# Four batch units in a row at the head of every round, in an interaction kernel with halved turns and double raw slots

## The reference

```python
e = jnp.stack([tbl_0[ids[:, 0]], ..., tbl_31[ids[:, 31]]], axis=1)
p = x[:, iu, :]
q = x[:, ju, :]
result = jnp.einsum('bpe,fpe,bpf->bp', p, kernel, q)
...
h = jnp.concatenate([z, dense_ctx], axis=1)
h = jnp.maximum(h @ W_top1 + b_top1, 0.0)
h = jnp.maximum(h @ W_top2 + b_top2, 0.0)
y = h @ W_top3
```

## Time and profile before

| | |
|---|---|
| runs | 496.06 us median of 3 (494.4 to 496.16) |
| the profiled execution | 494.39 us, span 492.6 us |
| TensorE, VectorE, ScalarE, GpSimd busy | 409.6, 355.8, 346.4, 241.9 us |
| VectorE's instructions | 367 |
| gathers | 256, 944 ns each |

### The profile page before, as it was taken

The page is one execution under the profiler, slowest core; times in us unless marked ns, Lnnn a source line. Parts: engine busy times, 40 slices in busy tenths (PEclk is TensorE's granted clock), DMA queues, the critical chain, the costliest instruction groups (busy, mean ns, idle before and its releaser), DMA issues.

```text
span 492.6 us, 8787 instructions
## 1 busy us (share of the span) xinstructions
PE 409.6 (83%) x2416; PEld 196.9 (40%) x2416; DVE 355.8 (72%) x367; ACT 346.4 (70%) x2661; POOL 241.9 (49%) x260
## 2 busy tenths in 40 slices
PE   0164999899797899999998899999998899999948
PEld 0031434343342444554333344644333354554226
DVE  0041899899786887659889886758988987668950
ACT  1000179989969859885997986789599689759802
POOL 5777777777027777771017777772017770000000
PEclk9995999999998999999999999999999999999979
DMA  3235354421001111110001111110001110000000
GB/s 93 77 102 174 98 183 150 130 53 29 3 6 27 26 28 27 28 27 8 2 5 28 28 28 25 27 28 13 1 5 27 28 28 3 0 2 3 0 1 0
DMA packets 11849, 19.16 MB, mean 39 GB/s; under 512 B 5013, under 2 KB 5913, under 8 KB 11673
## 3 DMA queue, kind: packets, MB, share of 16 engines
q0 software_dynamic: 8192, 8.40, 8.9%
q1 hardware_dynamic: 2592, 8.42, 4.8%
q10 hardware_dynamic: 1016, 1.78, 1.1%
HBM read 18.58 MB, written 0.00 MB: 38 GB/s over the span
## 4 chain that ended last, share of the span: by engine, by line
PE 38%; issue 20%; DVE 19%; ACT 10%; POOL 9%; DMA 2%; DVEq 0%; ACTq 0%; POOLq 0%
ACT prod_a L296 9%; POOL raw L250 9%; PE t_ps L437 9%; PE z_ps L493 8%; PE t_ps L515 6%; DVE prod_a L385 6%; PE t_ps L455 6%; DVE prod L359 4%; PE t_ps L523 3%; DVE zb L399 3%; PE prep_ps L469 2%; DMA raw<-tbl,ids_sb 2%; DVE prod_d L385 2%; PE t_ps L442 2%; DVE prod L363 2%
## 5 line engine op out<-in xcount | busy, mean ns | idle before, releaser
L250 POOL DMA_INDIRECT raw<-tbl,ids_sb x256 | 241.7, 944 | 164.4 <-issue 75.6
L296 ACT ACTIVATE prod_a<-prod_a 128x64 f32<-128x64 f32 x1296 | 309.4, 243 | 2.2 <-ACT y_sb L317 1.2
L296 ACT ACTIVATION_READ_ACCUMULATOR prod_a<-prod_a 128x1 f32 x1296 | 245.3, 189 | 0.0
L437 PE MATMUL t_ps<-xt,k_sb 64*128 64x256 f32 x448 | 129.2, 404 | 23.1 <-DVE prod_a L385 23.0
L359 DVE TENSOR_TENSOR prod<-t_ps,xt 128x1024 f32<-128x1024 f32 x96 | 116.3, 1212 | 41.2 <-PE t_ps L438 39.5
L455 PE MATMUL t_ps<-k_sb,xt 64*128 64x512 f32 x256 | 141.0, 632 | 0.6 <-issue 0.6
L457 PE MATMUL t_ps<-k_sb,xt 64*128 64x512 f32 x256 | 141.0, 632 | 0.0
L438 PE MATMUL t_ps<-xt,k_sb 64*128 64x256 f32 x448 | 129.2, 404 | 0.0
L437 PEld LDWEIGHTS t_ps<-xt,k_sb 64*128 64x128 f32 x448 | 77.9, 190 | 114.2 <-DVE prod_a L385 61.3
L385 DVE TENSOR_TENSOR prod_a<-t_ps,raw 128x1024 f32<-128x1024 f32 x81 | 97.9, 1209 | 0.0
L438 PEld LDWEIGHTS t_ps<-xt,k_sb 64*128 64x128 f32 x448 | 77.9, 190 | 0.0
(11 more groups left out here) (29 smaller groups left out, 216.8 us busy)
## 6 DMA issues: line engine op xcount, KB each, us to landing
raw<-tbl,ids_sb POOLq DMA_INDIRECT x256, 2.5
w_sb<-w ACTq DMA_DIRECT2D x1, 1024.0 KB
k_sb<-kmat SPq DMA_DIRECT2D x1, 992.0 KB, 7.0
k_sb<-kmat SPq DMA_DIRECT2D x1, 896.0 KB
k_sb<-kmat SPq DMA_DIRECT2D x1, 864.0 KB, 6.3
k_sb<-kmat SPq DMA_DIRECT2D x1, 768.0 KB, 4.2
k_sb<-kmat SPq DMA_DIRECT2D x1, 736.0 KB, 5.9
k_sb<-kmat SPq DMA_DIRECT2D x1, 640.0 KB, 4.3
```

Of the source, the lines that this page charges most:

```text
L250: nc.gpsimd.indirect_dma_start(raw[:, p % SLOTS, t, f * EMBED:(f + 1) * EMBED], None, tables[2 * k + f], bass.IndirectOffsetOnAxis(ap=ids_ ...
L296: last = nc.scalar.activation(prod_a[:, own, n, f, :], prod_a[:, own, n, f, :], ACT.Copy, accum_out=zb[:, q % 2, t, col + n * GF + f:col + ...
L437: nc.tensor.matmul(t_ps[:, slot, i, :], k_sb[0:EMBED, cols], xt[0:EMBED, x, :], start=True, stop=True)
```

## The change

The round's order: all batch units of a round stand ahead of its feature units. The batch units of quarter 3 are spread over rounds 25 to 31 (five in rounds 25, 26, 28 and 30), and round 32 is gone. The other parts: `raw` has two sets of 8 slots for packs 0 to 7 of a quarter and one set for packs 8 to 15, 24 in all as before; `xt` keeps its ring of 24. VectorE reduces 53 batch units instead of 47, ScalarE 75 instead of 81. A pair is due with the first unit that uses it, in quarters 2 and 3 a round earlier. A turn is made in two halves, after round 7 of its own quarter and after round 2 of the next one. For the last quarter, after the last selector sums, the first layer is made in four parts over all its outputs, with the second half of the turn between the third part and the fourth. Rows of `w1` are stored in the order of the parts.

```diff
@@ -13,7 +13,9 @@
...
 W = 2 * QB
-SLOTS = 24
+XRING = 24
+HELD = 2 * GROUP
+SLOTS = PACKS + HELD
 TRING = 3
@@ -67,16 +69,20 @@
...
+B_ALL = [("B", q, u) for q in range(QUARTERS) for u in range(NBU)]
+B_BEGIN = [BURST * max(0, r - 1) for r in range(LAST - ROUNDS + 2)]
+B_BEGIN += [B_BEGIN[-1] + -(-NBU * n // (ROUNDS - 1)) for n in range(1, ROUNDS)]
...
     out = []
-    for r in range(LAST + 1):
+    for r in range(LAST):
         q, at = divmod(r, ROUNDS)
-        feature = [("F", q, at * BURST + n) for n in range(BURST)] if r < LAST else []
-        q, at = divmod(r - 1, ROUNDS)
-        batch = [("B", q, at * BURST + n) for n in range(BURST)] if r else []
-        mixed = [x for n in range(BURST) for x in feature[n:n + 1] + batch[n:n + 1]]
-        out.append(mixed)
+        feature = [("F", q, at * BURST + n) for n in range(BURST)]
+        batch = B_ALL[B_BEGIN[r]:B_BEGIN[r + 1]]
+        out.append(batch + feature)
     return out
@@ -88,21 +94,31 @@
...
     n = q * NBU + u
-    return n % 3 == 0 or n >= QUARTERS * NBU - 6
+    return n % 5 in (0, 2) or n >= QUARTERS * NBU - 3
...
+def packs_of(unit):
+    kind, q, u = unit
+    k, ms = F_UNITS[u] if kind == "F" else (B_UNITS[u][0], ())
+    return [q * PACKS + x for x in ms + (k,)]
+FIRST_USE = {}
+for _r, _units in enumerate(ORDER):
+    for _x in _units:
+        for _p in packs_of(_x):
+            FIRST_USE.setdefault(_p // 2, _r)
...
-    q, at = divmod(r, ROUNDS)
-    if r >= LAST:
-        return []
-    last = F_UNITS[at * BURST + BURST - 1][0] // 2
-    first = F_UNITS[at * BURST - 1][0] // 2 + 1 if at else 0
-    return [q * PACKS // 2 + j for j in range(first, last + 1)]
+    return [j for j in sorted(FIRST_USE) if FIRST_USE[j] - (j >= PACKS) == r]
@@ -116,7 +132,8 @@
-TURN_ROUND, PIECE_ROUND = 2, 3
+TURN_ROUNDS, PIECE_ROUND = (ROUNDS - 1, ROUNDS + 2), 3
 PIECES = 4
@@ -125,13 +142,12 @@
...
     q, at = divmod(r, ROUNDS)
-    return (q - 1, at - PIECE_ROUND) if q and r < LAST and 0 <= at - PIECE_ROUND < PIECES else None
-def turned_after(r):
-    q, at = divmod(r, ROUNDS)
-    return q - 1 if q and r < LAST and at == TURN_ROUND else None
+    return (q - 1, at - PIECE_ROUND) if q and 0 <= at - PIECE_ROUND < PIECES else None
+def turns_after(r):
+    return [(q, c) for q in range(QUARTERS) for c in range(2) if q * ROUNDS + TURN_ROUNDS[c] == r]
@@ -216,7 +231,15 @@
...
+        def raw_slot(q, k):
+            return q % 2 * HELD + k if k < HELD else HELD + k
+        def raw_landed(q, k):
+            return 32 * BT * ((q // 2 if k < HELD else q) + 1)
@@ -239,18 +262,18 @@
...
                 q, k = divmod(p, PACKS)
-                if p >= SLOTS:
-                    before_q, before_k = divmod(p - SLOTS, PACKS)
-                    pool.wait_ge(prep_done, pair_copied(before_q, before_k))
-                    if before_k < 2 * GROUP:
-                        pool.wait_ge(prod_done, COUNT["B", before_q, NBU - 1])
+                if k < HELD and q >= 2:
+                    pool.wait_ge(prod_done, COUNT["B", q - 2, NBU - 1])
+                if k >= HELD and q:
+                    pool.wait_ge(prep_done, pair_copied(q - 1, k))
                 for f in range(2):
@@ -263,18 +286,18 @@
...
-            def copy_turned(q):
-                act.wait_ge(prep_done, PREP_COUNT["turn", q])
+            def copy_turned(q, c):
+                act.wait_ge(prep_done, PREP_COUNT["turn", q, c])
                 if q:
                     act.wait_ge(layer_done, piece_count(q - 1, 1))
-                nc.scalar.activation(zbt[:], prep_ps[:], ACT.Copy).then_inc(prep_copied, 1)
+                nc.scalar.activation(zbt[:, c, :], prep_ps[:, 0:QB], ACT.Copy).then_inc(prep_copied, 1)
@@ -462,21 +486,20 @@
...
+                for n in range(2):
...
-            def turn_sums(q):
-                pe.wait_ge(prep_copied, PREP_COUNT["turn", q] - 1)
-                pe.wait_ge(reduced_a, sum(x[0] <= q for x in SCALAR_UNITS))
-                pe.wait_ge(reduced_d, sum(x[0] <= q for x in VECTOR_UNITS))
-                for c in range(2):
-                    for t in range(BT):
-                        at = c * QB + t * P
-                        last = nc.tensor.transpose(prep_ps[:, at:at + P], zb[:, q % 2, t, c * P:(c + 1) * P], ident_sb[:])
+            def turn_sums(q, c):
+                last = (q, (c + 1) * NBU // 2 - 1)
+                pe.wait_ge(prep_copied, PREP_COUNT["turn", q, c] - 1)
+                pe.wait_ge(reduced_a, sum(x <= last for x in SCALAR_UNITS))
+                pe.wait_ge(reduced_d, sum(x <= last for x in VECTOR_UNITS))
+                for t in range(BT):
+                    last = nc.tensor.transpose(prep_ps[:, t * P:(t + 1) * P], zb[:, q % 2, t, c * P:(c + 1) * P], ident_sb[:])
                 last.then_inc(prep_done, 1)
@@ -500,20 +523,41 @@
...
+            def z_part(q, m, part):
+                slot, n = TURN_OF["piece", q, m // 2] % TRING, m % 2
+                z = zbt[:, part // 3, :] if part % 3 == 0 else zt[:, (part - 1) * QB:part * QB]
+                return nc.tensor.matmul(t_ps[:, slot, 2 * n, :], w1_sb[:, part, m * P:(m + 1) * P], z,
+                                        start=(part == 0), stop=(part == 3))
+            def last_layers(q):
+                for piece in range(2):
+                    take_turn(TURN_OF["piece", q, piece])
+                pe.wait_ge(prep_copied, PREP_COUNT["turn", q, 0])
+                for m in range(H1 // P):
+                    z_part(q, m, 0)
+                pe.wait_ge(z_copied, q + 1)
+                for part in (1, 2):
+                    for m in range(H1 // P):
+                        z_part(q, m, part)
+                turn_sums(q, 1)
+                pe.wait_ge(prep_copied, PREP_COUNT["turn", q, 1])
+                for m in range(H1 // P):
+                    z_part(q, m, 3).then_inc(layer_done, 1)
+                for piece in range(2, PIECES):
+                    layer(q, piece)
...
                     pe.wait_ge(z_copied, q + 1)
-                    pe.wait_ge(prep_copied, PREP_COUNT["turn", q])
+                    pe.wait_ge(prep_copied, PREP_COUNT["turn", q, 1])
                     if q == 0:
...
                 if piece < 2:
-                    for n in range(2):
-                        m = 2 * piece + n
-                        for t in range(4):
-                            z = zt[:, t * QB:(t + 1) * QB] if t < 2 else zbt[:, t - 2, :]
-                            last = nc.tensor.matmul(t_ps[:, slot, 2 * n, :], w1_sb[:, t, m * P:(m + 1) * P], z,
-                                                    start=(t == 0), stop=(t == 3))
+                    for m in (2 * piece, 2 * piece + 1):
+                        for part in range(4):
+                            last = z_part(q, m, part)
                         last.then_inc(layer_done, 1)
@@ -542,17 +586,16 @@
...
                     layer(*piece_after(r))
-                if turned_after(r) is not None:
-                    turn_sums(turned_after(r))
+                for q, c in turns_after(r):
+                    turn_sums(q, c)
                 for j in before_sums(r + 1):
...
                     transpose_pair(j)
-            turn_sums(QUARTERS - 1)
-            for piece in range(PIECES):
-                layer(QUARTERS - 1, piece)
+            feature_sums(LAST - 1)
+            last_layers(QUARTERS - 1)
```

More of the change, by code:

```diff
@@ L144, in prep_uses @@
     out = [("pair", j) for j in pairs_due(0)]
-    for r in range(LAST + 1):
-        if turned_after(r) is not None:
-            out.append(("turn", turned_after(r)))
+    for r in range(LAST):
+        out += [("turn",) + x for x in turns_after(r)]
         out += [("pair", j) for j in before_sums(r + 1) + after_sums(r + 1)]
-    return out + [("turn", QUARTERS - 1)]
+    return out + [("turn", QUARTERS - 1, 1)]
 PREP_COUNT = {use: n + 1 for n, use in enumerate(prep_uses())}
@@ L250, in _ @@
                         nc.gpsimd.indirect_dma_start(
-                            raw[:, p % SLOTS, t, f * EMBED:(f + 1) * EMBED], None, tables[2 * k + f],
+                            raw[:, raw_slot(q, k), t, f * EMBED:(f + 1) * EMBED], None, tables[2 * k + f],
                             bass.IndirectOffsetOnAxis(ap=ids_sb[:, q * BT + t, 2 * k + f:2 * k + f + 1], axis=0),
-                        ).then_inc(gathered[p % SLOTS], 16)
+                        ).then_inc(gathered[raw_slot(q, k)], 16)
         @block.scalar
@@ L324, in _ @@
                 copy_pair(j)
-            for r in range(LAST + 1):
+            for r in range(LAST):
                 if piece_after(r):
                     copy_layer(*piece_after(r))
-                if turned_after(r) is not None:
-                    copy_turned(turned_after(r))
+                for q, c in turns_after(r):
+                    copy_turned(q, c)
                 for j in before_sums(r + 1):
@@ L371, in batch_multiply @@
                 k, j, t = B_UNITS[u]
```

(6 more changed lines are left out.)

30 lines of the change are left out of this document (15 added, 15 removed).

## The result

| | before | with the change |
|---|---|---|
| time, median | 495.21 us (492.52 to 496.26, 16 runs) | 496.49 us (16 runs: 15 of 496.16 to 498.14, one of 2138.16) |
| profiled execution, its span | 494.39, 492.6 us | 496.26, 494.4 us |
| VectorE's end, and what follows | 475.28, 17.3 us | 477.37, 17.1 us |
| gaps, sum over rounds 1 to 30 (before: 31) | 75.7 us | 71.8 us |

The ratio is 1.0029, 95% interval 1.0017 to 1.0042: inside the 0.5% that the prediction called no change, and 496.49 where it said 496.5. The run of 2138.16 us stands outside the ratio, and why it was so slow isn't known. A gap is, as there, VectorE's idle time ahead of the first unit of a round.

A forecast was written before the change was run, and what follows sets the result against it. No engine is full, so VectorE's waits for TensorE's transforms at round ends bound it. Gaps -5.8 and VectorE's work +6.8 move its end +1.0; tail -0.1 makes +0.9. Forecast 496.5 us, range 490.5 to 501.5.

The forecast's parts named there:

- The sum: Whole kernel: gains and losses cancel, +0.9 us over the profiled run of 494.39, with a chance of 0.63.
- Lost covers, +10.2: Round ends: nine reductions of 1.13 us no longer keep VectorE working during TensorE's extra work, +10.2 us if nothing else changed.
- Gathers: GpSimd's loads no longer wait for a quarter's batch units; the gap after round 9, VectorE's longest wait at 5.0 us, becomes 0.
- Gaps: VectorE's idle time at the ends of rounds 1 to 30: 69.9 us against a comparable 75.7 before, -5.8.
- 1.15 to the end of the last transform: Price at each round end: TensorE's time from the slot's release by VectorE to the end of the round's last transform, 1.15 us.
- VectorE: +6.7 busy, forecast +6.8: VectorE's own work: 53 reductions instead of 47, six of 1.13 us, +6.8; with the gaps its end moves by +1.0.
- Tail: What follows VectorE's last instruction: 17.2 us, -0.1, the selector sums eating what the full clock and halved turn give.
- costed at nothing: ScalarE's six units fewer, 23 us less, count only where it is late for a copy; the gaps have no lateness in them.
- The rival of a late ScalarE: Slower: ScalarE comes late for copies TensorE needs sooner; four to six such places give 501 to 504 us; chance 0.20.
- its price of 1.35: Cost of each late ScalarE copy: turn to pair on TensorE took 2.70 us after round 18, unhindered 1.35, so 1.35 each.
- The Trainium skill's warning on TensorE: Short idling between matmul groups cycling through PSUM can swing the clock; the prediction found the trace doesn't bear it out.

The follow-up runs named there:

- 1: The changed kernel with feature and batch units alternating in a round again: 483.14 us, ratio to before 0.9766.
- 5: The changed kernel, same order and 53 reductions, dealt so that each round's last batch unit is VectorE's: 486.85 us, ratio to before 0.9825.
- 2: The kernel before with only the two sets of raw slots added: 492.06 us, ratio to before 0.9943.
- 9: The changed kernel with the last layers in the old order: 701.83 us on a chip where the kernel before took 765.74, so the time says nothing.
- 7: The changed kernel with the old sharing, 47 reductions on VectorE: 500.85 us, ratio to before 1.0126.
- 3: The kernel before with only the order inside a round changed, batch units first: 496.54 us, ratio to before 1.0038.
- 8: The changed kernel with whole, late turns and 47 reductions on VectorE: 501.29 us, ratio to before 1.0115.

## Why the prediction was right

**The number, in part luck.** The sum gave +0.9 over before. In the profiled executions it is +1.9 (494.4 for 492.6 of span), in the medians +1.3. The 496.5 stood 0.44 above a base of 496.06, the median of three runs; over 16 runs the base is 495.21 and the rise 1.28. The two errors, some 0.85 each, cancelled. What holds without luck is that gains and losses cancel.

**Lost covers, +10.2: shown in kind, priced a little high.** 1 and 5 give covers back in two ways, by order and by dealing alone. Eleven and ten more of them make the gaps 10.1 and 10.3 smaller, 0.9 to 1.0 each on average and 1.1 where the gap was long enough. At that rate the nine that were lost cost 8 to 9 us (an estimate); no run takes away just these nine.

**Gathers: right in the change, mis-sized as a term of its own.** All that was said is there: no gap after round 9, the queue on its step of 1.25 us, its only long wait just before 254 us for quarter 1's last batch unit, its last gather at 332.88. But 2 shows the 5 us of the gap were not there to be had by the slots alone: of them 4.2 came back after round 10 as ScalarE's lateness, and the 2.7 that the slots bring are mostly from rounds 17 and 25. The 5 us came free together with ScalarE's relief.

**Gaps: 71.8, forecast 69.9.** By quarter 7.1, 24.5, 22.9 and 17.3, forecast 6.5, 24.1, 22.3 and 17.0. By quarter the miss is small and one-sided. The term that was mis-sized is "1.15 to the end of the last transform", which was read behind a full unit; in 4 of the round ends of each quarter the last transform is a short one and ends some 0.1 later (behind round 16 the release is the short product's end, 256.55, and TensorE's next work starts at 257.81). The pieces' rounds leave 4.54 to 4.98 (forecast 4.4 to 5.2), rounds 8, 14, 15, 22 and 23 2.23, 3.02, 2.71, 3.03 and 2.72.

**VectorE: +6.7 busy, forecast +6.8; its end +2.1, forecast +1.0.** The gaps fell by 3.9 where 5.8 was forecast, 1.9 short. Of this 0.7 came back ahead of round 1, where VectorE waits 13.38 instead of 14.07, which the sum did not have. **Tail: 17.1, forecast 17.2**, at full clock. By 9 the parts of layer 1 save only 0.15 of it, and 1 shows what the order takes: 3.1 us.

**ScalarE "costed at nothing": the right outcome on too weak a reason.** The prediction took "VectorE's own work +6.8" as a loss, and ScalarE's 23 us less as worth nothing unless it is late. It is late without them: 7 gives the six units back to ScalarE, VectorE has 6.6 less to do and the gaps grow by 9.6, of which 5.6 are lateness. The rival of a late ScalarE was thus a real one, kept away by the new dealing, not by rounds long enough; its price of 1.35 was too low as well: after round 15 in 7 it is 3.8 with the half clock behind it. As the dealing belongs to the change, the sum held.

**Order and the rest, by runs.** 3 and 1 differ: the batch-first order costs 1.8 us in the old program and 13.3 in the new one. In the old one it also made two other stalls smaller, the gathers' and at four round ends ScalarE's, which the new program no longer has. (After round 10 it made ScalarE's larger.) In the new one only the loss was left, 3.1 of its 13.3 in the tail; the other parts had earned some 12 us (483.14 with units in turn against 494.78), and the order spent them all.

**Clock.** The Trainium skill's warning on TensorE, which the prediction weighed ("TensorE: Matmul & The Clock Gate", section "A second HAM failure mode: psum-queue depth-cycling"), isn't borne out after either: TensorE pauses at each round and the granted clock is 1.00 in all four quarters. In other kernels here it did fall at single places, behind a late copy in 2, 3, 7 and 8 and at the end of 5.
